# Attention kernel: the reciprocal of the softmax totals in three bf16 parts in place of two fp32r parts, spread by bf16 matmuls

## The reference

```
scores = einsum('bqhd,bkhd->bhqk', Qn, K) * SCALE + k_bonus
attn   = softmax(where(causal, -inf, scores), axis=-1)
out    = einsum('bhqk,bkhv->bqhv', attn, V).reshape(b, t, N_HEADS * D_VALUE)
return out @ W_out.T
```

## Time and profile before

| | |
|---|---|
| median of 3 runs | 1826.87 us (1824.72 to 1830.86) |
| the profiled execution | 1828.17 us, its span 1826.4 us |
| mean granted TensorE clock | 0.969 of 2.4 GHz |
| PE busy | 1664.5 us (91%) |
| DVE busy | 1356.9 us (74%) |
| POOL busy | 990.9 us (54%) |
| ACT busy | 890.1 us (49%) |

### The profile page before, as it was taken

How to read it: one execution, slowest core, us unless ns; L and a number is a source line. 1 busy time by engine, 2 the same in 40 slices (tenths; PEclk the granted TensorE clock), 3 DMA queues, 4 the chain that set the end, 5 groups by cost and what they waited for, 6 DMA issues and landing times.

```text
span 1826.4 us, 43279 instructions
## 1 busy us (share of the span) xinstructions
PE 1664.5 (91%) x12768; PEld 1245.9 (68%) x12768; DVE 1356.9 (74%) x4113; ACT 890.1 (49%) x2003; POOL 990.9 (54%) x1779
## 2 busy tenths in 40 slices
PE   3999999999999999975999999999999998669996
PEld 2676666676776666754778888888888886435553
DVE  6788888888888887764466777777777775648886
ACT  2665656665556665532444444444444443224443
POOL 5777777777777777752222333333333333227777
PEclk8999999999999999997999999999999999579998
DMA  1011111111111111201011000000000002434441
GB/s 41 10 38 42 52 52 52 52 52 52 44 34 52 52 52 52 81 13 41 12 58 58 30 30 30 30 29 29 29 29 29 29 24 88 155 105 134 130 134 44
DMA packets 78239, 95.76 MB, mean 52 GB/s; under 512 B 7046, under 2 KB 62995, under 8 KB 78160
## 3 DMA queue, kind: packets, MB, share of 16 engines
q1 hardware_dynamic: 70992, 77.91, 13.6%
q0 software_dynamic: 7168, 16.87, 2.6%
HBM read 53.14 MB, written 43.69 MB: 53 GB/s over the span
## 4 chain that ended last, share of the span: by engine, by line
PE 46%; DVE 3%; issue 2%; POOL 2%; ACT 1%; DMA 0%; DVEq 0%; POOLq 0%; SPq 0%; ACTq 0%
PE main L1243 7%; PE main L1245 6%; PE main L1252 6%; PE main L1431 4%; PE main L1269 3%; PE yp L1402 3%; PE xi L1219 3%; PE main L1386 2%; PE main L1389 2%; PE main L1387 2%; PE main L1290 2%; PE route L1445 1%; PE turn L1212 1%; PE xi L1445 1%; PE yp L1453 1%
## 5 line engine op out<-in xcount | busy, mean ns | idle before, releaser
L653 ACT ACTIVATE wgu<-score 128x384 f32<-128x384 f32 x512 | 223.2, 489 | 103.1 <-PE score L476 101.7
L498 PE MATMUL outp<-wgu 128*64 128x256 f32 (+1 forms) x2048 | 197.9, 336 | 29.8 <-POOL wgu L321 28.7
L321 POOL TENSOR_SCALAR_AFFINE_SELECT wgu<-wgu 128x512 f32<-128x512 f32 x256 | 167.1, 653 | 104.4 <-ACT wgu L653 92.1
L1243 PE MATMUL main<-hT_high,h_high 128*128 128x512 f32 x512 | 221.2, 432 | 0.9 <-ACT hT_high L1503 0.9
L1245 PE MATMUL main<-hT_high,h_low 128*128 128x512 f32 x512 | 201.3, 393 | 0.0
L498 PEld LDWEIGHTS outp<-wgu 128*64 128x64 f32 x2048 | 129.4, 138 | 89.5 <-issue 36.4
L1252 PE MATMUL main<-hT_low,h_high 128*128 128x512 f32 x512 | 138.4, 391 | 0.1
L792 DVE TENSOR_TENSOR wgu<-spread,wgu 128x512 f32<-128x512 f32 x128 | 88.5, 691 | 61.0 <-PE spread L520 46.3
L1843 DVE SCALAR_TENSOR_TENSOR th<-th,main 128x512 f32<-128x512 f32 x64 | 43.9, 686 | 114.0 <-ACT th L1570 114.0
L534 PE MATMUL back<-wout,wgu 128*128 128x128 f32 x1024 | 128.1, 279 | 0.0
L1219 PEld LDWEIGHTS xi<-state,wh_sb 128*128 128x128 f32 x512 | 93.8, 196 | 41.0 <-ACT state L1480 23.9
(11 more groups left out here) (272 smaller groups left out, 4299.7 us busy)
## 6 DMA issues: line engine op xcount, KB each, us to landing
sorted_d<-row_buf SPq DMA_DIRECT2D x26, 772.0 KB, 3.7
xg<-sorted_d SPq DMA_DIRECT2D x48, 386.0 KB, 3.1
wgu<-in_gate_up SPq DMA_DIRECT2D x4, 2048.0 KB, 9.4
xa<-in_x SPq DMA_DIRECT2D x32, 128.0 KB, 3.5
xr<-in_x SPq DMA_DIRECT2D x32, 128.0 KB, 3.2
x_d<-x SPq DMA_DIRECT2D x32, 128.0 KB, 1.9
x1c<-x_d SPq DMA_DIRECT2D x16, 256.0 KB, 2.8
x1v<-x_d SPq DMA_DIRECT2D x16, 256.0 KB, 2.8
```

The costliest lines, as they stand in the source:

```text
L321: pool.affine_select(out=blocks, in_=blocks, compare_op=ALU.is_ge, fill=0.0, base=0, pattern=[[0, 4], [1, P]], channel_multiplier=-1).then ...
L498: m = pe.matmul(outp[DV * i:DV * (i + 1), p % 2, k * P:T], val[par][:, k, h, :], weights(h, k), start=(k == 0), stop=(k == 1), tile_positi ...
L653: act.activation(prob[:, h // 2 % (RING // 2), :, h % 2, :], score[h % BANKS][:, 0:SC].rearrange("p (c q) -> p c q", q=P), ACT.Exp).then_i ...
L1243: pe.matmul(main[m % 2][:, :], w[0][:, k, m * P:(m + 1) * P], src[0][:, k, :], start=(k == 0), stop=False)
```

## The change

The reciprocal is split in three bf16 parts (high, middle, low) that sit on three groups of partitions. `rec_high` is now a bf16 copy of `rec`; `rec_rest` is what remains after the high part on the partitions of the middle and low parts; `rec_mid` is the bf16 copy of that; `rec_parts` subtracts it on the partitions of the low part, and is itself bf16. `back_to_r` becomes bf16 as well and picks three partitions for a head. The matmuls of `spread_out` keep their shape and number. The totals must lie on one more group of partitions, so `pick` gets a third diagonal; the matmuls that use it keep their shape. POOL writes three constants more, DVE makes two more small instructions in `constants()`.

```
-                for row, fill, base in ((high_row, 1.0, 0), (low_row, -1.0, -GROUPS)):
+                for row, fill, base in ((high_row, 1.0, 0), (mid_row, -1.0, -GROUPS), (low_row, -1.0, -2 * GROUPS)):
...
-                const(pool.memset(flat[:, GROUPS:GROUPS + GROUPS * (AUG + 1) - AUG:AUG + 1], 1.0))
-                const(pool.memset(pick[:, :, 2 * GROUPS:], 1.0))
+                for row in (GROUPS, 2 * GROUPS):
+                    const(pool.memset(flat[:, row:row + GROUPS * (AUG + 1) - AUG:AUG + 1], 1.0))
+                const(pool.memset(pick[:, :, 3 * GROUPS:], 1.0))
...
-        rec_high = sb("rec_high", [P, T], F32R)
-        rec_both = sb("rec_both", [P, T], F32R)
-        back_to_r = sb("back_to_r", [P, PAIRS_A, 2, DV], F32R)
+        rec_high = sb("rec_high", [P, T], BF16)
+        rec_rest = sb("rec_rest", [P, T])
+        rec_mid = sb("rec_mid", [P, T], BF16)
+        rec_parts = sb("rec_parts", [P, T], BF16)
+        back_to_r = sb("back_to_r", [P, PAIRS_A, 2, DV], BF16)
...
                 if g == 0:
-                    wait(pe, s["rec_both"], z + 1)
+                    wait(pe, s["rec_parts"], z + 1)
                 wait(pe, s["onT"], GROUPS * z + g)
                 for i in range(2):
                     m = pe.matmul(spread[:, i, :], back_to_r[:, 2 * g + i].rearrange("p i d -> p (i d)"),
-                                  rec_both[:], start=True, stop=True)
+                                  rec_parts[:], start=True, stop=True)
...
-                dve.tensor_tensor(back_row[:], high_row[:], low_row[:], ALU.subtract).then_inc(s["back_row"], 1)
+                dve.tensor_tensor(rest_row[:], mid_row[:], low_row[:], ALU.add).then_inc(s["rest_row"], 1)
+                dve.wait_ge(s["rest_row"], 1)
+                dve.tensor_tensor(back_row[:], high_row[:], rest_row[:], ALU.subtract).then_inc(s["back_row"], 1)
...
+                dve.tensor_reduce(rest_sel[:], rest_row[:], AX.X, ALU.add).then_inc(s["low_sel"], 1)
                 dve.tensor_reduce(low_sel[:], low_row[:], AX.X, ALU.add).then_inc(s["low_sel"], 1)
-                dve.wait_ge(s["low_sel"], 1)
+                dve.wait_ge(s["low_sel"], 2)
...
                 dve.tensor_copy(rec_high[:], rec[:]).then_inc(s["rec_high"], 1)
                 dve.wait_ge(s["rec_high"], z + 1)
-
-                dve.scalar_tensor_tensor(out=rec_both[:], in0=rec_high[:].bitcast(F32), scalar=low_sel[:, 0:1],
-                                         in1=rec[:], op0=ALU.mult, op1=ALU.add).then_inc(s["rec_both"], 1)
+                dve.scalar_tensor_tensor(out=rec_rest[:], in0=rec_high[:], scalar=rest_sel[:, 0:1], in1=rec[:],
+                                         op0=ALU.mult, op1=ALU.add).then_inc(s["rec_rest"], 1)
+                dve.wait_ge(s["rec_rest"], z + 1)
+                dve.tensor_copy(rec_mid[:], rec_rest[:]).then_inc(s["rec_mid"], 1)
+                dve.wait_ge(s["rec_mid"], z + 1)
+                dve.scalar_tensor_tensor(out=rec_parts[:], in0=rec_mid[:], scalar=low_sel[:, 0:1], in1=rec_rest[:],
+                                         op0=ALU.mult, op1=ALU.add).then_inc(s["rec_parts"], 1)
```

More of the change, by code:

```diff
@@ L117, in attention_layer @@
         back_row = sb("back_row", [P, HEADS])
+        mid_row = sb("mid_row", [P, HEADS])
         low_row = sb("low_row", [P, HEADS])
+        rest_row = sb("rest_row", [P, HEADS])
+        rest_sel = sb("rest_sel", [P, 1])
         low_sel = sb("low_sel", [P, 1])
@@ L197, in attention_layer @@
                  "qaug", "p_kaT", "p_qaT", "kaT", "qaT", "p_v", "val", "p_score", "prob", "masked", "p_out", "raw",
-                 "p_sum", "rec", "rec_high", "rec_both", "wv_split", "low_sel", "back_row", "back_r", "xnT_high", "xnT_low", "p_bc", "onT", "p_y",
+                 "p_sum", "rec", "rec_high", "rec_rest", "rec_mid", "rec_parts", "rest_row", "wv_split", "low_sel", "back_row", "back_r", "xnT_high", "xnT_low", "p_bc", "onT", "p_y",
                  "y", "stat_y", "mv_y", "yn", "xr", "x1", "x1_out", "mix_w", "mix_split_v", "mix_split_g", "mix_const", "blank", "fill")
@@ L205, in attention_layer @@
         N_IDENT = 4
-        N_CONST = 19
+        N_CONST = 22
         ctx.callback(clear, nc, list(s.values()))
```

## The result

The changed kernel takes 1822.97 us (median of 20 runs, 1819.16 to 1827.95), the kernel before in runs beside it 1828.08 (20 runs, 1824.67 to 1830.86). The ratio is 0.9975 [0.9967, 0.9983]: 5 us faster, 0.25%. The time lies in the predicted range, but it moved beyond its interval where I had forecast 1827 and no change, so the forecast of no change was wrong.

What follows compares the result with a forecast made beforehand. PE was taken to bound the attention loop. Loads -4.2, DVE stall +0.7, POOL +2.5, start +0.4 and end +0.85 sum to +0.25 us, giving 1827 us on the median of 1826.87; range 1818 to 1837.

Steps and rivals of the forecast that it cites:

- What bounds the kernel: Attention loop: PE, busy 46.26 of 48.59 us a turn; POOL's chain decides before the mask, PE's work behind it.
- The slower weight load: PE, spread_out 1 to 3 behind the mask: each bf16 load saves 0.05 us, 28 x 3 x 0.05 = -4.2 us.
- the sum: Whole kernel: -4.2 + 0.7 + 2.5 + 0.4 + 0.85 = +0.25 us.
- DVE: Two new instructions add 0.85 us a batch, mostly hidden; stalls before spread_out(z, 2) in 14 short steps cost +0.7 us.
- The slack at `spread_out(z, 0)`: Time from DVE's last part to PE's arrival: falls from 1.42 and 1.06 us to 0.57 (long step) and 0.21 (short).
- The idle time before `normalise(z, 1)`: On DVE: 0.9 us left in the long step and none in the short one.
- The wait before `spread_out(z, 2)`: PE waiting for DVE's normalise in the 14 short steps: mean 0.05 us each, together +0.7 us.
- POOL: Masks' chain, slowed by DVE's new instructions: 0.09 us a step, 28 x 0.09 = +2.5 us; bounds 0 and 0.28.
- Start and end: DVE's two new constants instructions before qkn cost +0.4 us; the last batch, where nothing covers DVE, costs +0.85.
- loads hide wholly: Rival, PE: exposed 0.12 us vanishes three times a step, -10.1 us, POOL isn't slowed: 1819 us; chance 0.17.
- full feedback from DVE: Within the rival "loads hide wholly": DVE takes back about 0.2 us in 14 short steps, 3 us, giving 1822.
- The turn: Attention loop, two steps: between 48.4 and 48.8 us if right; below 48.2 or above 49.0 if wrong.

Runs made afterwards that it cites:

- two bf16 parts: The kernel before with its two reciprocal parts and back_to_r in bf16 instead of fp32r, without the new DVE instructions: 1812.51 us, ratio 0.9925.
- three pauses: Three kernels: the kernel before with a useless DVE memset ahead of q5, of 128x32, 128x128 or 128x256: 1827.96, 1827.18 and 1826.75 us.
- shifted code: The kernel before with 56 one-column memsets added at the end of DVE's attention program: 1837.06 us, ratio 1.0052.
- the widest pause: The kernel before with a useless 128x256 memset on DVE ahead of q5: 1826.75 us, ratio 0.9998.
- Three fp32r parts: The changed kernel with its three reciprocal parts and back_to_r in fp32r instead of bf16: 1831.37 us, ratio 1.0025 to the kernel before.
- with the memset: The changed kernel with a useless 128x128 memset on DVE ahead of q5: 1830.97 us, ratio 1.0019 to the kernel before.

## Why the prediction was wrong, point by point

- **What bounds the kernel: right.** PE work before the mask was free (1822.75 against 1822.97) and behind it counted.
- **The slower weight load: right in mechanism and count, wrong in size. This is the step that failed.** "[T]he rows bound the load from above only, so I take 0.05." The exposed load went from 0.12 to nothing, three times a step, 0.11 on average: about -9 us in 26 to 28 batches instead of -4.2. That alone turns the sum from +0.25 into -4.8, near the 5.1 measured; but it is partly luck that it comes so near, as two terms that the sum didn't have, the first batch (about +1) and the clock's dip (-1.6), nearly cancel. Both ends were in the text (0.04 and 0.12), and I took the near one because a load behind a short matmul "needs some time in any case". The rows that bounded it, eight bf16 loads at 0.07 each in the earlier trace rows, show no more than the pace of their eight matmuls, which is the same 0.07 (the timeline of PE after the change, 513.80 to 514.34):

```profile
513.80 0.61 PE L564 MATMUL turned<-ident_b,k_aug 128*128 128x128 bf16 x8
514.34 0.34 PE L482 MATMUL score<-q_augT,k_augT 32*128 32x256 bf16 x4
```

  They say nothing on what remains exposed. The Trainium skill, TensorE: Matmul & The Clock Gate, section Weight-path perf modes, has the fast weight load on for 128 weights of a type that isn't FP32, about twice as fast. The records agree, 189 to 98 ns, if fp32r is counted with the slow type, which the page doesn't say. The same page of the Trainium skill, section Step-by-step: what each phase is for, says that loads are pulled ahead of matmuls in flight. It doesn't say what stays exposed: here 0.09 to 0.12 us of a 189 ns load and nothing of a 98 ns one.
- **DVE: right, a little low.** 0.85 a batch was forecast. The long step shows it (0.84); in the short one `rec_parts` is stretched to 0.73 beside the mask, 1.1 in all. The slack at `spread_out(z, 0)`, forecast 0.57 and 0.21, is 0.58 in the long step; in the short one there is none, and PE waits 0.12. The idle time before `normalise(z, 1)` is 0.53 where I had 0.9, and none in the short step. The wait before `spread_out(z, 2)` came out as forecast in place, 0.07 to 0.1 instead of 0.05.
- **POOL: the size was right, the picture too simple.** 0.18 a turn was forecast, 0.19 measured in one pair of profiles and 0.30 in the other. In the first it is the sum of a long step that is 0.08 shorter and a short step that is 0.27 longer, and against two bf16 parts, whose loads are as short, the two instructions cost POOL 0.49 a turn. So the near hit is partly luck: two changes of opposite sign add up to it. Of the 0.73 us in which `rec_parts` lies beside a mask and `k_part`, some 0.54 was lost on the two engines together; of the overlap of `rec_rest` with POOL's line 380 in the long step, 0.14 of 0.28, as in the earlier trace rows. The rule of the Trainium skill (SBUF — State Buffer, Who interferes with whom) that one waits out the other is nearer to the first than to the second, and in the first both engines' instructions grew.
- **Start and end:** +0.85 at the end as forecast; at the start +1.5 and +0.4 in the two pairs, in place of +0.4. The forecast had only the constants (PE's first `spread_out` comes 0.59 and 0.06 later) and left out the first batch, where DVE's slack is small too: PE waits 0.44 and 0.24 for `normalise` there and reaches the fourth `spread_out` 1.81 and 0.67 later.
- **The rival "loads hide wholly"** came nearest, with its 1822 at full feedback from DVE. That feedback was too large (0.2 for a short step, where about 0.1 was measured), and its other half, that POOL isn't slowed, doesn't hold; the two errors cancel in part. Without the two DVE instructions there are the 1812.51 of two bf16 parts.
- **The turn** is 48.20, at the border of what I had called wrong (below 48.2). Of the two causes named there one holds, the hidden loads; the overlaps weren't harmless.

Two bf16 parts beat both kernels, by 9 to 10 us the one with three; what it gives up is the third part's precision in the reciprocal.

## What to carry to other kernels

An exposed operation can save all of its exposed time when it gets shorter, and not only a part by the ratio of the durations (here 0.12 of 0.12, with the record halved): measure the exposed time from start to next start, and let a load of half the length count as hidden unless a row of that type behind the same short work shows otherwise. Work added to an engine with little slack was paid for mostly through a neighbour, here POOL's masks, and the next piece of the same size cost three times as much. When a forecast comes out right, compare its terms too: here two missing terms nearly cancelled, and the two steps of POOL moved in opposite directions. A few more instructions can slow a stage far from them by more than the edit is worth, so read the time of each stage, not only the total.

## What the runs showed of the hardware that I had not expected

**A dip of the clock in the steady part, seen only with fp32r parts.** One long step of the profiled execution before took 26.2 us instead of 24.6. The windows view of that step's work behind the mask, and of the same work one turn earlier (the eighth column is the granted clock):

```profile
704.70:708.70 4.00, 3.92 (x34) 2.29 (x36) 1.32 (x3) 0.60 (x1) 2.33 (x5) 0.57 0.00 0
656.20:660.20 4.00, 3.99 (x46) 2.90 (x47) 2.19 (x4) 1.77 (x5) 2.63 (x6) 1.00 0.00 0
```

A mean of 0.57 is mostly the lower of the two levels, 1.2 GHz in place of 2.4. PE's timeline shows what stood before it, the long wait of 1.30 us for the mask, and the 16 matmuls at 2.68 us instead of 1.52:

```profile
704.78 2.68 PE L498 MATMUL outp<-wgu 128*64 128x256 f32 x16 [1.30 <-POOL wgu L321]
```

In the steady part each of the six profiles of kernels with two fp32r parts (before twice, three pauses, shifted code) has such a step (five have one, the widest pause two), always behind the mask wait of a long step (1.27 to 1.30). Three fp32r parts have three, behind waits of 1.20 and 1.21. The seven profiles with bf16 parts have none, though in three of them (the changed kernel twice and with the memset) PE waits as long at that place as with three fp32r parts, 1.19 to 1.23. The cost is 1.6 us each. bf16 parts don't keep the clock up everywhere: near the end of the attention both kernels have such a fall (16 matmuls take 2.83 us at 800.67 in the kernel before, 2.24 at 796.08 in the changed one). Why the type should matter is open; only the count is shown.

**Two engines, two kinds of overlap.** An overlap of a DVE and a POOL instruction cost anything from nothing (`rec_parts` beside POOL's line 383 in the long step, 0.48 and 0.26 us as without it) to about three quarters of its length (0.54 of 0.73), and the same chain of 10 us took 9.8 or 10.1 from kernel to kernel and from step to step.
